# Decoder layer, one core: another order in the drain of self-attention

## The reference

```python
def attn(x):                      # 16 heads of 128, causal
    k, q, v = (einsum('ihd,bpd->biph', W, x) for W in (W_K, W_Q, W_V))
    s = einsum('biph,biqh->biqp', k, q)
    a = softmax((s * tril - 1e10 * (1 - tril)) / sqrt(128))
    return einsum('df,bqf->bqd', W_O, (a @ v).transpose(0, 2, 1, 3).reshape(b, pos, -1))
def xattn(q, c, gamma):           # 8 heads of 64 rows; keys and values are both ctx
    a = softmax(qh.T @ ch / sqrt(64)); return gamma * (a @ ch.T)
def ffn(x):                       # ternary weights, activations quantised to 127 steps
    xq = quant(norm(x)); return (silu(xq @ sign(W_g).T) * (xq @ sign(W_u).T)) @ sign(W_d).T
x = layernorm(x + attn(x)); x = layernorm(x + xattn(x, ctx, gamma)); x = layernorm(x + ffn(x))
```

## Time and profile before

| | us |
|---|---|
| median of three runs | 1494.51 |
| the profiled execution, its own time | 1496.47 |
| its span, first to last instruction | 1494.7 |
| mean granted TensorE clock, share of full speed | 0.983 |

### The profile page before, as it was taken

The page is one execution under the profiler, slowest core; times in us unless marked ns, Lnnn a source line. Parts: engine busy times, 40 slices in busy tenths (PEclk is TensorE's granted clock), DMA queues, the critical chain, the costliest instruction groups (busy, mean ns, idle before and its releaser), DMA issues. The chain is left out here.

```text
span 1494.7 us, 23730 instructions
## 1 busy us (share of the span) xinstructions
PE 1438.2 (96%) x7008; PEld 1149.2 (77%) x7008; DVE 1071.8 (72%) x2324; ACT 716.8 (48%) x1535; POOL 653.1 (44%) x507
## 2 busy tenths in 40 slices
PE   7999999999999999999999999878998989999996
PEld 6788888888888888888888888757787865565564
DVE  4667677776777676767776767677787895796854
ACT  3444444535444444444444444356787863333332
POOL 1343525334344344352444352566767543343432
PEclk9999999999999999999999999989999998999999
DMA  7466666666666666566566665744456613000000
GB/s 193 134 182 183 179 177 176 193 162 179 172 182 177 175 175 186 158 190 182 169 174 180 184 177 156 217 135 106 128 136 163 175 43 113 1 29 28 0 29 28
DMA packets 205034, 213.97 MB, mean 143 GB/s; under 512 B 98752, under 2 KB 172480, under 8 KB 204992
## 3 DMA queue, kind: packets, MB, share of 16 engines
q1 hardware_dynamic: 203840, 212.93, 51.1%
q10 hardware_dynamic: 1152, 0.52, 0.2%
HBM read 125.83 MB, written 79.69 MB: 138 GB/s over the span
## 5 line engine op out<-in xcount | busy, mean ns | idle before, releaser
L667 ACT ACTIVATE probs<-probs,neg_max 128x128 f32<-128x128 f32 (+3 forms) x256 | 142.4, 557 | 357.8 <-DVE neg_max L796 350.3
L475 POOL TENSOR_TENSOR v_lo<-placed,v_hi 128x512 fp32r<-128x512 f32 x63 | 81.9, 1299 | 350.7 <-ACT v_hi L673 350.7
L477 POOL TENSOR_TENSOR pT_lo<-placed,pT_hi 128x1280 fp32r<-128x1280 f32 x63 | 186.5, 2960 | 0.0
L856 DVE SCALAR_TENSOR_TENSOR acc<-bank,prob_recip,acc 128x512 f32<-128x512 f32 x256 | 174.8, 745 | 6.0 <-PE bank L560 1.1
L1521 POOL TENSOR_TENSOR prod_lo<-prod,prod_hi 128x512 fp32r<-128x512 f32 x64 | 84.5, 1320 | 143.3 <-ACT prod_hi L1630 143.3
L796 DVE CUSTOM_DVE_ANT_0 probs<-bank,mask 128x128 f32<-128x128 f32 (+3 forms) x256 | 117.1, 481 | 8.2
L771 DVE TENSOR_TENSOR qT_lo<-bank,qT_hi 128x512 fp32r<-128x512 f32 x64 | 44.2, 691 | 104.8 <-ACT qT_hi L655 104.8
L1073 POOL TENSOR_SCALAR xprobs<-xprobs,xprob_recip 128x512 f32<-128x512 f32 x128 | 87.4, 703 | 69.5 <-DVE xprob_recip L1294 69.5
L808 DVE STREAM_TRANSPOSE turned<-probs 128x256 f32<-128x256 f32 (+1 forms) x384 | 114.0, 363 | 0.0
L1580 PE MATMUL bank<-wdT_f32r,prod_hi 128*128 128x512 f32 x256 | 109.9, 429 | 2.1 <-POOL prod_lo L1521 1.6
L1223 ACT ACTIVATE xprobs<-bank,xneg_max 128x512 f32<-128x512 f32 x128 | 88.9, 695 | 43.8 <-DVE xneg_max L1283 42.9
(11 more groups left out here) (159 smaller groups left out, 3862.9 us busy)
## 6 DMA issues: line engine op xcount, KB each, us to landing
turned_scratch<-turned SPq DMA_DIRECT2D x64, 896.0 KB, 3.8
placed<-turned_scratch SPq DMA_DIRECT2D x252, 224.0 KB, 4.2
cp<-context_halves SPq DMA_DIRECT2D x64, 256.0 KB, 3.9
context_halves<-ctx_halves SPq DMA_DIRECT2D x16, 512.0 KB, 4.9
xs<-rows_pair SPq DMA_DIRECT2D x60, 128.0 KB, 3.6
acc<-in_x_dram SPq DMA_DIRECT2D x16, 256.0 KB, 4.9
rows<-in_L_attn_W_V_dram SPq DMA_DIRECT2D x64, 64.0 KB, 2.2
rows<-in_L_attn_W_O_dram SPq DMA_DIRECT2D x64, 64.0 KB, 2.7
```

The costliest lines, as they stand in the source:

```text
L477: nc.gpsimd.tensor_tensor(pT[par][1][:], landed_probs(landing), pT[par][0][:].bitcast(F32), ALU.subtract).then_inc(p_lo, 1)
L667: nc.scalar.activation(probs[:, cols], probs[:, cols], ACT.Exp, bias=low[:, par, t:t + 1], scale=-1.0, accum_out=total[:, par, t:t + 1]).t ...
L856: nc.vector.scalar_tensor_tensor(out=acc[:, b * NT + t, :], in0=s_bank[t][:], scalar=recip[:, b, t:t + 1], in1=acc[:, b * NT + t, :], op0= ...
```

## The change

Five edits, all in the drain:

1. SP: the four loads of context tiles into `rows` are no longer issued together after the last exchange of head 14. They go one or two at a time into the exchanges of that head (batches 1, 2 and 3), between write and reads, ahead of the loads that stand there.
2. SP: the rows of W_u for head 15 are issued behind item 62's write instead of behind its reads.
3. ACT: z_hi of item 62 comes before the halves of item 63 instead of behind them.
4. PE and DVE: scores and maximum of unit 2 come before item 63's output product and its additions. PE's wait for v's last transposition stands ahead of item 62's `values_product`.
5. The first ten units' scores go over four banks (1, 2, 3, 0) instead of two. So unit v from 4 on waits for the exponential of v-4.

```diff
         def loads(h, b, more):
 
+            if not more:
+                for name in {1: ("wk", "wq"), 2: ("wv",), 3: ("wo",)}.get(b, ()) if h < H - 1 else ():
+                    sp.wait_ge(w_turn[name], H)
+                    rows.load_tile(sp, 0, tuple(raw).index(name))
...
-        for t, name in enumerate(("wk", "wq", "wv", "wo")):
-            sp.wait_ge(w_turn[name], H)
-            rows.load_tile(sp, 0, t)
         loads(H - 1, 0, False)
-        exchange(FIRST + 2, 0, landing=1)
-        loads(H - 1, 1, False)
+        exchange(FIRST + 2, 0, lambda: loads(H - 1, 1, False), landing=1)
         loads(H - 1, 2, False)
...
+        pe.wait_ge(v_turn, ITEMS)
         values_product(FIRST + 2, 2, Z_BANK[2])
-        pe.wait_ge(v_turn, ITEMS)
...
-        for unit in range(2):
+        for unit in range(3):
             cross.scores(pe, unit)
         output_product(FIRST + 3, 1)
-        for unit in range(2, 8):
+        for unit in range(3, 8):
...
+        z_hi_of(2)
         halves_hi(FIRST + 3, 1)
-        z_hi_of(2)
...
-        for unit in range(2):
+        for unit in range(3):
             cross.row_max(dve, unit)
...
+    BEGIN_BANKS = (bank[1], bank[2], bank[3], bank[0])
+    def bank_of(v):
+        return BEGIN_BANKS[v % 4] if v < S_AHEAD else score_bank[v % 2]
...
-        if v > 1:
+        if v >= S_AHEAD:
             pe.wait_ge(exp_done, v - 1)
+        elif v >= 4:
+            pe.wait_ge(exp_done, v - 3)
...
-        for v in range(2, S_AHEAD):
+        for v in range(3, S_AHEAD):
             row_max(dve, v)
```

More of the change, by code:

```diff
@@ L1134, in scores_tile @@
         for p in range(2):
-            last = nc.tensor.matmul(score_bank[t % 2][:], xs[h % 2][:, t * P:(t + 1) * P], cp[h % 2][:, p, :],
+            last = nc.tensor.matmul(bank_of(v)[:], xs[h % 2][:, t * P:(t + 1) * P], cp[h % 2][:, p, :],
                                     start=(p == 0), stop=(p == 1))
@@ L1222, in exp_tile @@
         act.wait_ge(max_ready, v + 1)
-        nc.scalar.activation(probs[q][:, t, :], score_bank[t % 2][:], ACT.Exp, bias=negmax[:, q, t:t + 1],
+        nc.scalar.activation(probs[q][:, t, :], bank_of(v)[:], ACT.Exp, bias=negmax[:, q, t:t + 1],
                              accum_out=total[:, q, t:t + 1]).then_inc(exp_done, 1)
@@ L1282, in tile_max @@
         dve.wait_ge(scores_full, v + 1)
-        nc.vector.tensor_reduce(negmax[:, q, t:t + 1], score_bank[t % 2][:], AX.X, ALU.max, negate=True).then_inc(max_ready, 1)
+        nc.vector.tensor_reduce(negmax[:, q, t:t + 1], bank_of(v)[:], AX.X, ALU.max, negate=True).then_inc(max_ready, 1)
     def row_max(dve, v):
```

## The result

| | before | after |
|---|---|---|
| median, same session (4 executions each) | 1494.84 (1493.49 to 1496.28) | 1483.46 (1482.44 to 1484.68) |
| ratio, 95% interval | | 0.9924 [0.9907, 0.9941] |
| profiled execution, span / own time | 1494.7 / 1496.47 | 1480.6 / 1482.44 |
| mean granted clock of that execution | 0.983 | 0.992 |

The account below looks back on a forecast made before the run. The prediction took one chain across engines in the drain as the bound, with the second reciprocal dating the restart. 5.2 us up to the last addition plus 1.8 for banks made 7.0: 1494.51 to 1487.5 us, range 1483.5 to 1492.0.

Parts of the forecast that it names:

- from z of item 62 to the last addition: End of self-attention: engines alternate and PE's clock stays as before, so the gain stays 5.2 us.
- z of item 62: DVE's low half of z for item 62 in the drain: 5.2 us earlier, at 968.3.
- SP's loads, write to reads: SP's queue in the drain: item 62's reads follow its write after 4.4 us, so come 3.8 us earlier.
- the rival of 7.07: Item 62's write lands as slowly as before, 7.07 us: gain only 4.3 us, 1490.2; chance 0.15.
- the swap's share: ACT taking z_hi of item 62 before item 63's halves: worth 1 us of the 5.2.
- a return of the clock for item 62's product: Bound: 2.5 us more if its twelve products run at full clock; as a rival 1485.0, chance 0.12.
- Banks, and unit 2 moved: Last addition to second reciprocal: 7.1 us of DVE work instead of 8.9 us, gain 1.8.
- DVE not waiting for PE in between: Expected profile sign: seven us from last addition to second reciprocal, without DVE waiting for PE.
- The upper bound of 3.6 us: Most the bank term could gain from last addition to second reciprocal, if DVE had no other work.
- Everything behind shifted alike: Behind the second reciprocal, POOL's tiles, DVE and PE come earlier by as much, 7.0 us.
- Tile loads in head 14: Loads moved into head 14's exchanges cost nothing, with 3.7 us of cover; rival that they make it slower: chance 0.04.
- The median lay 1.96 below that execution: 1494.51 - 7.0: Conversion of the profiled execution's 1489.5 us to a forecast median of 1487.5 us.

Follow-up runs that it names:

- e1: Kernel before with only SP's two edits (context tile loads moved, W_u's rows behind item 62's write): 1488.4 us, ratio 0.9969.
- e2: Kernel before with SP's two edits and ACT's new order, without the banks and unit 2's move: 1487.7 us, ratio 0.9967.
- e7: Kernel after with ACT's old order, halves of item 63 ahead of z_hi of item 62: 1484.58 us, ratio 0.9954 to before.
- e6: Kernel after with unit 2's scores and maximum again behind item 63's output product, four banks kept: 1486.65 us, ratio 0.9971 to before.
- e5: Kernel after, unchanged, run again beside the kernel before: 1484.2 us, ratio 0.9953.
- e9: Kernel after plus twelve matrix products of no use ahead of item 62's output product: 1482.67 us, ratio 0.9948 to before.
- e8: Kernel after with DVE's statistics of batch 1 moved earlier and two of POOL's four tiles normalised by DVE: 1480.07 us, ratio 0.9922 to before.
- e10: e9 plus nine more products of no use ahead of cross-attention's first transposes: 1483.58 us, ratio 0.9942 to before.
- e11: e8 with the second reciprocal and batch 1's variance ahead of unit 8's maximum on DVE: 1480.78 us, ratio 0.9933 to before.
- e12: e11 with both sets of products of no use from e10: 1477.72 us, ratio 0.9919 to before.
- e4: Kernel before, unchanged, as a control with a second profile: 1493.27 us, ratio 1.001.
- e3: Kernel before with only the four banks, unit 2 and PE's wait moved; SP and ACT as before: 1491.06 us, ratio 0.9992.

## Why the prediction was right in kind and too small

The step that failed is the one from z of item 62 to the last addition: it was priced without any change of its own, and it gave 1.8 us of its own. Gains from the key half on, after against before, beside the forecast:

- *SP's loads, write to reads:* 4.29 us, forecast 4.4; the rival of 7.07 is out. Item 62's last scores complete 2.3 earlier (2.4). Right, and e1 shows SP's edits doing it alone.
- *z of item 61:* 4.1 (3.8). *z of item 62:* 5.6 (5.2). Right in sum, and for the swap's share by luck: its 1 us was no part of it (e2, e7). Without the swap item 63 landed 0.7 us sooner behind its write than assumed, and DVE was still adding.
- *From z of item 62 to the last addition: the step that failed.* "The new gaps of 3.4 and some 1.7 us (a third score fills 0.4 of it) lie near these, so I price it as before: gain stays 5.2". It was 7.4 us. The mis-sized term is the clock. Item 62's product left the low level before its end (967.97 to 972.43, 4.5 us; before 974.29 to 979.58, 5.3): 0.8 us, the greater part of what z of item 62 to z of item 63 lost (11.5 to 10.5). So it is in all nine profiles with a gap of 3.2 to 3.5 us ahead of it (4.2 to 4.5 us), and not in the two of before with 4.4 and 4.8 (5.3 us). Item 63's product ran at 2.4 GHz, 1.5 us less; DVE's additions lost their 1.4 us of waits by it (4.1 to 2.7), of which the third maximum ahead of them took 0.6, so 0.8 came through. With 0.4 that z of item 62 already had over the forecast, 1.0 and 0.8 make the 2.2. I bounded a return of the clock for item 62's product only and priced it at nothing, left out item 63's product although the trace before has it at 0.58 of the clock, and gave the third score in front of item 63's no effect but 0.4 us of filler; e6 puts 0.8 to 1.0 of the 2.2 on that score.
- *Banks, and unit 2 moved:* 1.8 in the profile of after, as forecast and by the forecast's own sum: DVE works through six maxima and the statistics. But "DVE not waiting for PE in between" held in one of three profiles: in e5 and e7 it is 7.85 us from addition to reciprocal rather than 7.0, from a wait that the prediction did not have, POOL's first normalising, and the low clock behind it. The banks alone gave none of it (e6). The upper bound of 3.6 us comes out of no row: PE's five waits there are 3.1. Unit 2's move, with what it does to item 63's product, is worth 2.5 us by the medians (e6 against e5).
- *Everything behind shifted alike:* reciprocal to restart is 12.5 us in all eleven profiles whose border is not edited. Right. *Tile loads in head 14* cost nothing: the three exchanges take 6.57, 6.94 and 7.54 us from write to reads, before 6.54, 6.94 and 7.55, and no wait of PE appeared there.
- *"The median lay 1.96 below that execution: 1494.51 - 7.0".* The other error. The reference was three executions, and its four in the result's comparison had a median of 1494.84; 75 executions of the same kernel over the three sessions of experiments have a mean of 1492.1, with a standard deviation of 2.3. Those of after (12) have 1484.2. The difference of means is 7.9 us, with some 1.2 either way, and e5 beside its own before has 7.0; so of the measured 11.4 about 7 to 9 are the change and the rest is which executions were drawn. The range had a term for every cost in the drain and none for this. Its lower end is also not the sum of its own bounds: 1485.0 less the bank term's 1.8 is 1483.2, not 1483.5 (and the upper one would be 1490.4 + 1.8 = 1492.2). That the time lies 0.04 us outside says little; that the drain gave 9.1 us instead of 7.0 says what was wrong.

What stays open: why e9's product fell to the low level at a gap of 1.95 us and those of e8, e10, e11 and e12 at 2.09 to 2.25 did not, and whether the 2 us between the restarts of the profiles (9 us earlier) and e5's ratio (7.0 us, with an interval from 4.6 to 9.4) are anything.

## What to carry to other kernels

Where a chain alternates between engines, price a matmul group behind an idle time at both clock levels, for every such group, and count work moved in front of it as more than its own length: here the scores of one unit ahead of a group went with 1.5 us less in it, though not in every run. Work off the chain's end (here POOL's tiles, shared out) before work in its waits: what is taken out of a wait leaves the wait. And a forecast range for a fraction of a per cent needs the spread of the reference itself, which three executions don't show.

## What the runs showed of the hardware

- One kernel's single executions run from 1488.4 to 1498.0 us over three chips, and the time goes with the mean granted clock of the execution: correlation -0.78 over 75, about 0.9 us for 0.001 of clock.
- The low level came after idle times as short as 1.95 to 2.45 us, and at other times did not: 2.2 us ahead of the feed-forward stood once before a group that took 1.87 us, and once before the same group at 1.06.
- Products of no use needn't cost time, and may pay: e12 is e11 with 21 more matmuls and 3 us less, of which the profiles place 1.6; e9 and e10 gained nothing that their times tell. The Trainium skill, TensorE: Matmul & The Clock Gate, section "What's actually happening", has it that the low clock is the default and activity releases it. Item 62's product in e9, behind twelve such products, agrees: granted 1.00, where after had 0.50.
- The reads that wait for item 62's 896 KB write followed it after 4.3 us in after, and after 4.2 to 4.9 in the ten runs with SP's edits, with four loads of W_u queued behind it; with four context tiles (1 MB) ahead of it they followed after 7.07 us, 6.7 in e4 and 6.4 in e3.
